# Edge one-hots of both layers made from broadcast rows of edge numbers, relation scores of layer 1 as matmuls in its edge phase, and no masking of running counts, in a two-layer GNN with feed-forward blocks

## What is computed

```python
# 1: GNN layer 0, 4 heads of 64 features; src is the node that sums, dst the neighbour
score = a_s[src] + a_d[dst] + aw_e * elem + ab          # a_s, a_d: products of the node features
w = exp(-relu(score / 20))
out[n] = sum over edges with src == n of w * feats[dst]  /  the sum of w
# 2: 16 experts, top-2 per node, silu(x w1) * (x w2), then w3
# 3: GNN layer 1; dst is the node that sums, src the neighbour
W = (W3 @ a)[:, 0]; w_src, w_dst, w_rel = W[:256], W[256:512], W[512:]
score = h[src] @ w_src + h[dst] @ w_dst + rel_emb[etype] @ w_rel
alpha = exp(leaky_relu(score)); alpha = alpha / alpha
out[n] = relu(sum over edges with dst == n of ((h[src] + rel_emb[etype]) @ weight_neighbor) * alpha)
         + h @ loop_weight            # evolve_loop_weight where no edge comes in
# 4: per batch, the top half of the rows through a 256 -> 1024 -> 256 block
```

## Time and profile before

| | |
|---|---|
| median of 3 runs | 2573.14 us (2571.25 to 2574.58) |
| the profiled execution | 2573.98 us |
| its span | 2572.2 us |
| mean granted clock of TensorE in it | 0.841 |
| busy: PE, DVE, ACT, POOL | 1832.3, 1918.8, 685.5, 1349.8 us |
| L895, gathers of both edge phases | 952 x 945 ns = 900.1 us |
| DMA packets | 168883, 314.64 MB |

### The profile page before, as it was taken

How to read it: one execution, slowest core, us unless ns; L and a number is a source line. 1 busy time by engine, 2 the same in 40 slices (tenths; PEclk the granted TensorE clock), 3 DMA queues, 4 the chain that set the end, 5 groups by cost and what they waited for, 6 DMA issues and landing times. The chain is left out here.

```text
span 2572.2 us, 40237 instructions
## 1 busy us (share of the span) xinstructions
PE 1832.3 (71%) x10390; PEld 1358.9 (53%) x10390; DVE 1918.8 (75%) x4736; ACT 685.5 (27%) x2162; POOL 1349.8 (52%) x1250
## 2 busy tenths in 40 slices
PE   0799367777777734399999974466766666667997
PEld 0698234444444424389999972343433333335776
DVE  8997887777777776599999726677777777566395
ACT  0000122222222212011111112444444444334331
...
GB/s 94 2 4 16 50 89 106 106 107 106 107 106 107 99 38 51 151 252 260 260 260 260 260 198 148 90 159 158 158 157 158 157 158 157 128 60 35 27 0 50
DMA packets 168883, 314.64 MB, mean 122 GB/s; under 512 B 31712, under 2 KB 91868, under 8 KB 168668
## 3 DMA queue, kind: packets, MB, share of 16 engines
...
...
HBM read 287.49 MB, written 25.95 MB: 122 GB/s over the span
## 5 line engine op out<-in xcount | busy, mean ns | idle before, releaser
L895 POOL DMA_INDIRECT e_rows<-table,e_gidx x952 | 900.1, 945 | 312.1 <-issue 255.1
L1145 PE MATMUL e_psO<-e_rows,wide_oh 128*128 128x260 f32 x928 | 364.0, 525 | 141.5 <-DVE acc L947 140.5
L947 DVE TENSOR_TENSOR acc<-acc,e_psO 128x260 f32 (+1 forms) x708 | 349.8, 494 | 34.3 <-PE e_psO L1145 3.0
L1145 PEld LDWEIGHTS e_psO<-e_rows,wide_oh 128*128 128x128 f32 x928 | 191.5, 241 | 276.7 <-DVE acc L947 253.0
L1895 PE MATMUL e_psO<-e_rows,e_oh 128*128 128x456 bf16 x488 | 219.4, 450 | 134.5 <-ACT e_oh L1842 113.7
L1842 ACT ACTIVATE e_oh<-e_oh,inverse 128x128 bf16<-128x128 bf16 x488 | 155.8, 389 | 111.4 <-DVE inverse L1858 110.4
L611 POOL DMA_INDIRECT records<-ordered,s_chunk x68 | 121.9, 1793 | 118.9 <-ACT ordered L604 103.1
L597 PE MATMUL sort_ps<-work 125*104 125x64 f32 x850 | 151.4, 382 | 21.6 <-DVE work L587 15.6
L927 DVE TENSOR_TENSOR e_oh<-seg,e_psI 128x512 bf16<-128x512 f32 x238 | 162.5, 683 | 2.3 <-issue 0.4
L1897 PE MATMUL e_psO<-e_rows,e_oh 128*128 128x256 bf16 x488 | 163.2, 334 | 0.0
L1896 PE MATMUL e_psO<-e_rows,e_oh 128*128 128x256 bf16 x488 | 162.9, 334 | 0.0
...
...
## 6 DMA issues: line engine op xcount, KB each, us to landing
...
e_rows<-table,e_gidx POOLq DMA_INDIRECT x952, 2.8
...
```

What stands on the lines that cost most here:

```text
L895: pool.indirect_dma_start(out=rows[:, r, t, 0:width], out_offset=None, in_=table, in_offset=bass.IndirectOffsetOnAxis(ap=gidx[:, r, t:t + ...
L947: v.tensor_tensor(d, d, psO[:, units * (r % (4 // units)) + j, 0:accw], ALU.add).then_inc(S["added"], 1)
L1145: return pe.matmul(out[:, 0:A0], wide[:, r, t, :], rows[:, r, t, :], start=start, stop=stop)
```

## The change

**One-hots from rows.** Each sort's `number_rows` takes the loaded records, before `unpack`, and writes as bf16, for each edge tile, a line of the 128 row numbers (and, in layer 1, a line of the 128 relation types); SP stores it to `edge_rows` in DRAM and waits. In the edge phases SP, which had nothing to do there, broadcasts 4 lines to all 128 partitions for each group (`erow`). DVE compares them with the partition's number (`unumber`): this gives `ohT` directly (L978 of the new file). The PE transposes, their PSUM and ACT's copy are gone. `oh` is made by four TENSOR_SCALAR of 128x128 with `seg`'s column as the scalar and an iota in SBUF (L984): f32 in layer 0, so that ACT's widening goes too, bf16 in layer 1. The relation counts are four TENSOR_SCALAR of 128x200 (L1809).

**Relation scores in the edge phase.** In layer 1 DVE also makes `ohR`, the turned one-hot of the type in two parts (128 and 72 types), and PE adds, behind each of the four matmuls into `psA`, two more of 3 columns with `relcol`: the 200 scores in three bf16 terms. `relcol` is made in the stage of the third layernorm, by 8 small matmuls and 10 small DVE instructions. The 425 SCALAR_TENSOR_TENSOR, `relrow`, `relwb`, their matmul, `relscore1` and L1799's addition are gone, and layer 1's records have 2 fields.

**No masking.** POOL's multiplication of the counts is gone. `select` in layer 1 instead gets the steps of the running count (`run` less `run` one column before), by one copy of a column and two more TENSOR_TENSOR per block, in the place of L564.

```diff
-    FIELDS = (2, 3)
+    FIELDS = (2, 2)
+    KINDS = (1, 2)
...
-            if self.ends is None:
+            if hot is None:
                 link(v.tensor_tensor(picked, picked, self.hot[:, blocks, :, :], ALU.mult))
             else:
-                link(v.scalar_tensor_tensor(picked, self.run[:, blocks, :, :], 0.0, picked, ALU.is_gt, ALU.mult))
+
+                runs = self.flat_run[0:EP, k * NB * CB:(k + 1) * NB * CB]
+                steps = hot.rearrange("p b c -> p (b c)")
+                v.tensor_copy(steps[:, 0:1], runs[:, 0:1])
+                link(v.tensor_tensor(steps[:, 1:], runs[:, 1:], runs[:, 0:NB * CB - 1], ALU.subtract))
+                link(v.tensor_tensor(picked, picked, hot.unsqueeze(1), ALU.mult))
...
+        def number_rows(self, dve, link, lines, rowi, rowb):
+
+            v = nc.vector
+            dve.wait_ge(self.landed, 16)
+            field = lines[:, :, :].rearrange("p g (e f) -> p g e f", f=self.nf)
+            link(v.tensor_copy(rowi, field[:, :, :, 0]))
+            link(v.tensor_scalar(rowi, rowi, PIECE.bit_length() - 1, None, ALU.arith_shift_right))
+            ins = v.tensor_scalar(rowb[:, :, 0, :], rowi, -1.0, None, ALU.add)
+            if KINDS[self.l] > 1:
+                ins = v.tensor_copy(rowb[:, :, 1, :], field[:, :, :, 1])
+            ins.then_inc(self.rowed, 1)
+
+        def store_rows(self, sp, rowb):
+            sp.wait_ge(self.rowed, 1)
+            sp.dma_start(seg_d[self.l].rearrange("(g p) w -> p g w", p=P),
+                         rowb[:, :, :, :].rearrange("p g k e -> p g (k e)")).then_inc(self.row_stored, 16)
+            sp.wait_ge(self.row_stored, 16)
...
+                    back(sp, S["ohT_ready"], g, DEPTH)
+                    sp.dma_start(erow[:, r, :, :, :].rearrange("p t k e -> p (t k e)"),
+                                 seg_d[l][bass.ds(g * TPG, TPG), :].rearrange("t w -> (t w)").partition_broadcast(P))\
+                        .then_inc(row_landed[r], 16)
...
+                    dve.wait_ge(row_landed[r], q * 16 + 16)
+
+                    back(dve, S["own_e"], g, 2)
+                    hold(dve, "dve")
+                    if l:
+                        for k, n in ((0, P), (1, R - P)):
+                            v.tensor_scalar(ohR[0:n, r % 2, k, :, :], erow[0:n, r, :, 1, :], unumber[0:n, k:k + 1], None,
+                                            ALU.is_equal)
+                    v.tensor_scalar(ohT[:, r % 2, :, :], erow[:, r, :, 0, :], unumber[:, 0:1], None, ALU.is_equal)\
+                        .then_inc(S["ohT_ready"], 1)
+
                     back(dve, S["summed"], g, DEPTH)
-                    v.tensor_tensor(oh[:, r, :, :], seg[l][:, bass.ds(g * TPG, TPG)].unsqueeze(2).to_broadcast([P, TPG, P]),
-                                    psI[:, 0:P].unsqueeze(1).to_broadcast([P, TPG, P]), ALU.is_equal)\
-                        .then_inc(S["oh_ready"], 1)
+                    hold(dve, "dve")
+                    for t in range(TPG):
+                        ins = v.tensor_scalar(oh[:, r, t, :], (iota_b if l else iota)[:, 0:P],
+                                              seg[l][:, bass.ds(g * TPG + t, 1)], None, ALU.is_equal)
+                    ins.then_inc(S["oh_ready"], 1)
...
-                    if nxt is not None:
-                        g, q, r = nxt
-                        act.wait_ge(S["turned"], g + 1)
-
-                        back(act, S["own_e"], g, 2)
-                        nc.scalar.activation(ohT[:, r % 2, :, :].rearrange("p t n -> p (t n)"), psT[:, :],
-                                             ACT.Copy).then_inc(S["ohT_ready"], 1)
...
-                            ins = pe.matmul(psA[:, r % na, t * 3 * heads:(t + 1) * 3 * heads], ohT[:, r % 2, t, :],
-                                            seen[:, :, bass.ds(g * units + t // tpu, 1)]
-                                            .rearrange("p k a -> p (k a)"), start=True, stop=True)
+                            out = psA[:, r % 2, t * 3 * heads:(t + 1) * 3 * heads]
+                            ins = pe.matmul(out, ohT[:, r % 2, t, :], seen[:, :, bass.ds(g * units + t // tpu, 1)]
+                                            .rearrange("p k a -> p (k a)"), start=True, stop=(l == 0))
+                            if l:
+                                pe.matmul(out, ohR[:, r % 2, 0, t, :], relcol[:, 0, :], start=False, stop=False)
+                                ins = pe.matmul(out, ohR[0:R - P, r % 2, 1, t, :], relcol[0:R - P, 1, :], start=False,
+                                                stop=True)
                         ins.then_inc(S["own_e"], 1)
-                    if nxt is not None:
-                        g, q, r = nxt
-                        pe.wait_ge(S["oh_ready"], g + 1)
-
-                        back(pe, S["ohT_ready"], g, 1)
-                        for t in range(TPG):
-                            ins = pe.transpose(psT[:, t * P:(t + 1) * P], oh[:, r, t, :], ident_b[:, :])
-                        ins.then_inc(S["turned"], 1)
...
-            def l0_widen(act, at, oh, S):
-
-                g, q, r = at
-                act.wait_ge(S["oh_ready"], g + 1)
-                if not isinstance(g, int) or g >= DEPTH:
-                    act.wait_ge(S["summed"], g - (DEPTH - 1))
-                hold(act, "act")
-                nc.scalar.activation(wide[:, r, :, :], oh[:, r, :, :], ACT.Copy).then_inc(S["widened"], 1)
...
-                    pool.wait_ge(ends_kept, 1)
-                    nc.gpsimd.tensor_tensor(flat_run[0:EP, :], flat_run[0:EP, :], flat_hot[0:EP, :], ALU.mult)\
-                        .then_inc(masked, 1)
-                    pool.wait_ge(masked, 1)
...
-                            for c in range(lo, hi):
-                                ins = v.scalar_tensor_tensor(
-                                    relpick[c % len(relpick)], iota[0:EP, :], es1.field[:, c, 1:2], relrow[0:EP, :],
-                                    ALU.is_equal, ALU.mult, accum_out=es1.field[:, c, 2:3])
-                            ins.then_inc(rel_scored, 1)
...
+                        dve.wait_ge(rel_p, 2)
+                        for b, n in ((0, P), (1, R - P)):
+                            value, rest = relcol_f[0:n, b, 0:1], relcol_f[0:n, b, 1:2]
+                            link(v.tensor_copy(value, dn.psF[0:n, 1, b:b + 1]))
+                            link(v.tensor_copy(relcol[0:n, b, 0:1], value))
+                            link(v.tensor_tensor(rest, value, relcol[0:n, b, 0:1], ALU.subtract))
+                            link(v.tensor_copy(relcol[0:n, b, 1:2], rest))
+                            link(v.tensor_tensor(relcol[0:n, b, 2:3], rest, relcol[0:n, b, 1:2], ALU.subtract))
+                        dve.sem_inc(rel_kept, 1)
...
+                        for b, n in ((0, P), (1, R - P)):
+                            for j in range(KD):
+                                ins = pe.matmul(dn.psF[0:n, 1, b:b + 1], relT[:, j, b * P:b * P + n],
+                                                wcol[:, 2 * KD + j:2 * KD + j + 1], start=(j == 0), stop=(j == KD - 1))
+                        ins.then_inc(rel_p, 1)
+                        pe.wait_ge(rel_kept, 1)
...
-                v.tensor_tensor(rows[:, r, :, :].bitcast(BF16)[:, :, T1:T1 + R], etype1[:, bass.ds(g * TPG, TPG)].unsqueeze(2).to_broadcast([P, TPG, R]),
-                                psI[:, 0:R].unsqueeze(1).to_broadcast([P, TPG, R]), ALU.is_equal)\
-                    .then_inc(S["counted"], 1)
...
+                counts = rows[:, r, :, :].bitcast(BF16)
+                for t in range(TPG):
+                    ins = v.tensor_scalar(counts[:, t, T1:T1 + R], iota_b[:, :], etype1[:, bass.ds(g * TPG + t, 1)], None,
+                                          ALU.is_equal)
+                ins.then_inc(S["counted"], 1)
...
-                dve.wait_ge(steps, g + 1)
-                v.tensor_tensor(s, s, mine[:, r % 2, :].unsqueeze(2), ALU.add).then_inc(own_summed, 1)
```

127 lines of the change are left out of this document (56 added, 71 removed).

## The result

The changed kernel takes 2587.23 us (median of 4 runs, 2583.54 to 2590.03), the kernel before beside it 2573.76 (4 runs). The ratio is 1.0053, with a 95% interval of 1.0036 to 1.0071: slower by 13.5 us, where 2558 was forecast. The profiled execution is the fastest of the four, 2583.54, with a span of 2581.8: 9.6 above the span before.

| piece | before | after | moved | predicted |
|---|---|---|---|---|
| start to layer 0's first gather | 322.88 | 323.72 | +0.8 | C +1.5 |
| layer 0's gathers | 591.48 | 591.44 | 0.0 | E -4, F +2, part of G |
| to the first w3 tile | 174.02 | 154.78 | -19.2 | A -18.95 |
| first to last w3 tile | 441.48 | 424.99 | -16.5 | B -10.4 |
| to layer 1's first gather | 121.30 | 124.50 | +3.2 | D +2.8 |

A forecast was written before the change was run, and what follows sets the result against it. POOL's gathers were taken to bound both edge phases, at 5.00 us a group. Terms A -18.95, B -10.4, C +1.5, D +2.8, E -4, F +11, G +3 sum to -15.05, giving 2558 us; range 2540 to 2602.

The forecast's parts named there:

- C: End of the first stage: layer 0's `number_rows` adds three DVE instructions ahead of `unpack`, +1.5 us.
- E: Start of layer 0's gathers: index copy moved ahead, so gathers 9 to 12 go without a wait, -4 us.
- F: New DVE instructions in the edge phases: DVE no bound, some gathers slowed; +9 layer 1, +2 layer 0, +11 us together.
- G: SP's row broadcasts in the edge phases: more DMA load, hidden except in the last groups, +3 us.
- A: No masking: the first L1238 no longer stands still beside POOL's multiplication, -18.95 us.
- B: Expert stage: relation row's matmul and PE's waits for DVE go, L597's fewer columns give 0; -10.4 us.
- D: Stage of the third layernorm: ten small DVE instructions and eight one-column matmuls before the first `mix`, +2.8 us.
- Rival 1: Edge phases: new DVE instructions shut POOL's gathers out, +73 us layer 1, +12 layer 0, total 2632; chance 0.16.
- Rival 2: Layer 1: new DVE instructions run one element at a time, DVE 5.5 us a group, total 2616; chance 0.07.
- rival 3: Layer 1: DMA becomes the bound if short broadcast packets cost twice their bytes, 2580 to 2598; chance 0.05.
- sign set for rival 2: Edge phases: DVE's idle time for gathered rows, otherwise over 0.5 us a group, vanishes and POOL waits for PE instead.

The follow-up runs named there:

- early alpha: Changed kernel with layer 1's `oh` and counts as TENSOR_TENSORs between the TENSOR_SCALARs, and alpha made before anything for later groups: 2550.12 us, ratio 0.9904.
- parted kernel: Changed kernel with layer 1's `oh` and counts as one TENSOR_TENSOR each, iota in PSUM, separating the three TENSOR_SCALARs left: 2589.08 us, ratio 1.0051.

## Why the prediction was wrong

*A, right.* -19.2 against -18.95; the four instructions of L1238 take 7.40 in one row of the timeline, and the expert stage begins that much earlier. *C and D, right:* +0.8 and +3.2 against +1.5 and +2.8.

*B, right in kind, under-sized:* -16.5 against -10.4. The two long waits shrank to one of 1.48. What I had not counted are the tiles behind them. Fourteen times the starts of two w3 tiles were 5.69 us apart where it is 5.52 now, and fourteen times 10.20 where it is 10.08; near the end one was 7.30 and is 5.52. So "Later in the stage PE runs without a gap" was false by some 4 us, and 1.8 more at the end: delays of 0.12 and 0.17 us are too short to be listed as waits. L597 with 64 columns gave nothing, as said: 4.71 for 50, where 96 columns take 4.74 in an undisturbed round.

*E, right at its start.* The ninth gather starts at once and the thirteenth at 344.24 where it was 347.59. The tenth and eleventh were stretched, beside DVE's edge terms (two TENSOR_TENSORs of 128x1856 f32 in SBUF, from 334.39 to 339.80). The timeline of POOL:

```profile
334.20 0.95 POOL L940 DMA_INDIRECT e_rows<-table,e_gidx  x1 [0.31 <-issue]
335.45 3.05 POOL L940 DMA_INDIRECT e_rows<-table,e_gidx  x1 [0.30 <-issue]
338.81 1.82 POOL L940 DMA_INDIRECT e_rows<-table,e_gidx  x1 [0.30 <-issue]
...
344.24 0.94 POOL L940 DMA_INDIRECT e_rows<-table,e_gidx  x1 [2.36 <-ACT e_gidx L1035]
```

The last groups of layer 0 gave the rest back: the last 40 gathers start 1.36 us apart on average where it was 1.30, some 2.5 us in all. That is *G*, which I had priced only for layer 1's end; there it is some 3 us over the last 40 gathers, as forecast. Without the broadcasts both ends are back at 1.29 and 1.50 (1.30 and 1.53 before).

*F is the step that failed.* It put layer 1 at +9, and layer 1's gathers took 41.3 us more. Its own sign said so: a mean gather of 973 ns or more was to make the change no gain, and it is 985. It failed in three places.

First, the size of DVE's own part. "3 x 0.20 + 4 x 0.11 + 4 x 0.13 = 1.56" measured 2.25. I had taken 0.07 us for each start, and it is 0.13: bf16 instructions of 128, 200 and 512 elements follow each other at 0.163, 0.181 and 0.263 us, that is 0.13 us and 0.26 ns for each element, and f32 ones of 128 at 0.196, which is twice that slope with the same 0.13. By the Trainium skill, VectorE: DVE Perf Modes, "The perf-mode tier table", tensor_scalar handles four bf16 or two f32 elements where the slowest mode handles one; the spacings agree, and my reading of the earlier trace rows as one element a nanosecond was wrong. DVE's work became 4.2 us a group instead of 3.6.

Second, "neither is a bound" looked at the engines' shares alone. 4.2 of 5.00 us is no bound for DVE, but it stands in a round: DVE's own sum to alpha, ACT's scaling (1.3), PE's product (1.7 at the full clock, 3.3 at the lower), the own sums behind it, and DVE again, two groups later. The one-hots stand between the score and alpha, so each 0.1 us there counts in the round. PE's product waits 167.1 us for ACT in 1700 to 2200 us where it waited 86.7, the granted clock of the phase is 0.75 where it was 0.83, and the product takes longer. How much the clock adds was not separated, nor what lowers it: with the early alpha PE waits 184.3 us for ACT and the clock is 0.79. The parted kernel showed this holder alone, the early alpha removed it. It was in the trace of before: DVE stood idle 38.2 us before L1806, 32.3 of them for PE, while POOL was the bound.

Third, the stretch. "One gather in four so met, 122 x 0.08 = +9" measured +33.3 (35.4 the second time). It is not one in four by 0.08 but one in five (93 of 488 take over 1 us) by 0.35. It goes by where in the chain a gather starts: the 39 that start within 0.22 us of the first TENSOR_SCALAR end 0.07 to 0.46 late, the 30 that start 0.37 to 0.76 us behind it 0.48 to 0.64 late, and those that start 0.82 to 0.95 behind it take 0.951 on average. At the start of the counts' chain of four, 20 of 59 take over 1 us, and nearly all others are less than 0.02 late. Rival 1 named this mechanism; its chance was too low (0.16) and its price, +73 in layer 1, twice what came. Its rule from the Trainium skill (SBUF — State Buffer, "Who interferes with whom": the second to issue is blocked for the other's whole length) agrees in kind with the trace, and is not borne out for gathers that start 0.82 us or more into a chain of 1.56. Layer 0, where the chain is one bf16 and four f32 instructions, had 5.0 us of stretch, of which 3.0 fell beside the edge terms, 0.5 on the first gather and 1.5 behind them: F's +2 was right there.

*Rival 2* (one element at a time) and *rival 3* (DMA) are excluded, by the spacings and by the run without broadcasts. Half of the sign set for rival 2 came true all the same: DVE's wait for gathered rows is gone (2.0 us in 500). It told of the round, not of slow instructions; POOL's wait for PE, the other half, is 6.6 us. What the forecast could not have said is that two holders stood at nearly the same height. It could have said that the round had 0.6 us less slack than it counted.
